# Cross-attention with a gated feed-forward layer: the second feed-forward weight converted in the second softmax stage by three engines, awaited chunk by chunk, and two slots of the attention output chain moved

## The reference

```
qh = (LN(x) @ Wq.T)    # 32 heads of 16; kh, vh from ctx: 8 groups, each used by 4 heads
attn = softmax(qh @ kh.T / 4)
x = x + (attn @ vh) @ Wfc.T + bfc
y = LN(x)                                     # fp8 (e4m3) products from here on
act = gelu(y @ w_gating[0]) * (y @ w_gating[1])   # 512 -> 2048, twice
out = x + act @ w_linear                      # 2048 -> 512
```

## Time and profile before

| | us |
|---|---|
| median of 3 runs | 476.73 |
| lowest and highest of them | 475.73, 479.82 |
| the profiled execution | 478.06 |
| its span, first to last instruction | 476.3 |

### The profile page before, as it was taken

One profiled execution on the slowest core, in us unless ns is written; L12 is line 12 of the kernel. 1 busy time (PEld: TensorE's weight loads), 2 busy tenths in 40 slices (PEclk: granted clock), 3 DMA queues, 4 the chain that ended last, 5 costly groups with the idle time before them and its releaser, 6 DMA issues.

```text
span 476.3 us, 11726 instructions
## 1 busy us (share of the span) xinstructions
PE 431.6 (91%) x4592; PEld 345.2 (72%) x4592; DVE 332.7 (70%) x688; ACT 314.6 (66%) x578; POOL 242.0 (51%) x227
## 2 busy tenths in 40 slices
PE   2977855889999999999999999999999999888997
PEld 2846744667797778877887778877887788557973
DVE  4587582886789667975888677966797578365442
ACT  5749862886459774787469755877479745775541
POOL 5679951589116950398027920696029810592000
PEclk9977977799999999999999999999999999899999
DMA  8878569653430454025601552034501250000001
GB/s 282 290 218 316 155 186 247 166 170 101 127 76 2 103 142 112 3 53 149 156 3 27 144 133 59 2 93 132 135 3 47 68 133 27 3 23 23 2 24 45
DMA packets 21720, 49.80 MB, mean 105 GB/s; under 512 B 5152, under 2 KB 5664, under 8 KB 21664
## 3 DMA queue, kind: packets, MB, share of 16 engines
q1 hardware_dynamic: 21376, 48.25, 36.0%
q10 hardware_dynamic: 288, 0.79, 0.6%
HBM read 23.86 MB, written 4.19 MB: 59 GB/s over the span
## 4 chain that ended last, share of the span: by engine, by line
PE 64%; DVE 10%; POOL 10%; issue 5%; DMA 4%; SPq 4%; ACT 3%; POOLq 0%; ACTq 0%; DVEq 0%
PE bank L627 17%; PE bank L647 10%; PE bank L435 7%; PE bank L436 6%; PE bank L437 6%; POOL plo L1242 6%; PE bank L538 5%; PE bank L505 4%; DMA stage<-in_w 3%; DVE mneg L1040 3%; PE bank L462 2%; PE bank L556 2%; PE bank L558 2%; SPq L349 2%; DVE osum L1053 1%
## 5 line engine op out<-in xcount | busy, mean ns | idle before, releaser
L1242 POOL TENSOR_TENSOR plo<-p,phi 128x512 f16<-128x512 f32 x128 | 152.6, 1208 | 49.5 <-ACT phi L822 49.0
L627 PE MATMUL bank<-x2T,wgate 128*128 128x128 fp8e4 x2048 | 130.9, 221 | 0.8 <-ACT x2T L834 0.8
L627 PEld LDWEIGHTS bank<-x2T,wgate 128*128 128x128 fp8e4 x2048 | 117.6, 99 | 14.2 <-issue 7.1
L1040 DVE TENSOR_REDUCE mneg<-bank 128x4 fp32r<-128x512 f32 x128 | 85.1, 685 | 21.3 <-PE bank L505 20.8
L819 ACT ACTIVATE p<-bank 128x512 f32<-128x512 f32 x128 | 77.6, 606 | 28.3 <-PE bank L538 27.6
L822 ACT ACTIVATE phi<-bank 128x512 f16<-128x512 f32 x128 | 77.5, 605 | 0.0
L647 PE MATMUL bank<-wlin,act 128*128 128x512 fp8e4 x256 | 74.4, 387 | 0.0
L845 ACT CAST ff<-bank 128x512 bf16<-128x512 f32 x64 | 37.4, 584 | 48.7 <-PE bank L627 48.7
L505 PE MATMUL bank<-kmask,cq 128*128 128x512 f32 x128 | 57.4, 480 | 6.1 <-DVE mneg L1040 5.4
L538 PE MATMUL bank<-qs,ks 98*128 98x512 f32 x128 | 55.1, 430 | 4.4 <-DMA qs<-mrow 2.5
L841 ACT ACTIVATE gate<-bank 128x512 bf16<-128x512 f32 x64 | 38.2, 597 | 31.1 <-PE bank L627 30.2
(11 more groups left out here) (111 smaller groups left out, 817.3 us busy)
## 6 DMA issues: line engine op xcount, KB each, us to landing
qs<-cq SPq DMA_DIRECT2D x90, 128.0 KB, 2.5
stage<-in_w SPq DMA_DIRECT2D x17, 512.0 KB, 6.3
ks<-khl SPq DMA_DIRECT2D x96, 64.0 KB, 2.0
cin<-in_ctx SPq DMA_DIRECT2D x8, 512.0 KB, 4.1
xr<-in_x SPq DMA_DIRECT2D x16, 256.0 KB, 3.7
out<-xr SPq DMA_DIRECT2D x16, 256.0 KB, 2.5
xr<-in_w SPq DMA_DIRECT2D x5, 512.0 KB, 4.6
kmask<-khl SPq DMA_DIRECT2D x28, 64.0 KB, 2.0
```

The source lines that it names most:

```text
L627: mm = pe.matmul(out[:, h * SEQ:(h + 1) * SEQ], wgate8[:, UH * v + h, kk, part, :], x2T[:, b % NB, kk, :], start=kk == 0, stop=kk == KT - 1)
L1040: dve.tensor_reduce(dst[:, :, 2 * half:2 * half + 2, j].rearrange("p a r -> p r a"), bank_of("S", q, i, s)[:, :].rearrange("p (r a k) -> p ...
L1242: pool.tensor_tensor(plo[:, e % PBUF, :], p32[:, e % P32BUF, :], phi[:, e % PBUF, :], ALU.subtract).then_inc(plo_ok, 1)
```

## The change

- Chunks 21 to 28 are converted in the softmax stage of pair 1: 21, 23, 25 and 27 by DVE at slots 3, 5, 8 and 11; 22, 24, 26 and 28 by POOL at slots 3, 5, 8 and 11 and by ACT two slots behind. The feed-forward part of pair 0 has no clamps and casts any more. Counts of conversions stay 11 by DVE and 13 by POOL and ACT.
- `down` of batch 0 waits at each slot for the chunk that it reads, and no longer for all.
- Places: chunks 17 to 28 go to `g0`, `g1`, `st0`, `st1`, then `st2`, `x6`, `st0`, `st1` twice.
- SP loads chunk 21 behind the context of pair 2, 22 to 24 behind all Q copies, and 25 to 28 in pair 1 ahead of `mask_k`.
- In pair 0 DVE converts its last two chunks a slot earlier (13 and 15), and `norm2_apply` and `turn_x2` come a slot earlier (17 and 18).
- In the last pair `turn_x2` and `x2_out` of batch 13 come at slot 14 and not at 11.

```diff
-W_PLACE += [("st0", "st1", "st2", "x4", "x6")[n % 5] for n in range(W_LIN - len(W_PLACE))]
-W_PLACE += [("st0", "st1", "st2")[n % 3] for n in range(CHUNKS - W_LIN)]
-W_DVE = [8, 10, 12, 14, 16, 18, 20] + list(range(W_LIN + 4, CHUNKS))
+W_PLACE += ["st0", "st1", "st2", "x4", "x6", "g0", "g1", "st0", "st1"]
+W_PLACE += [("st2", "x6", "st0", "st1")[n % 4] for n in range(CHUNKS - W_LIN)]
+W_DVE = [8, 10, 12, 14, 16, 18, 20] + list(range(W_LIN, CHUNKS, 2))
-CLAMP_SLOTS = (2, 5, 8, 10, 12, 14, 16)
-DVE_SLOTS = ((3, 5, 7, 9, 11, 14, 16), (1, 3, 5, 7))
+CLAMP_SLOTS = ((2, 5, 8, 10, 12, 14, 16), (3, 5, 8, 11))
+DVE_SLOTS = ((3, 5, 7, 9, 11, 13, 15), (3, 5, 8, 11))
-CHAIN_E = {True: dict(turn=13, project=(14, 14, 15, 15), residual=16, rstd=16, norm=17, turn2=19),
+LAST_TURN2 = 14
+CHAIN_E = {True: dict(turn=13, project=(14, 14, 15, 15), residual=16, rstd=16, norm=16, turn2=18),
...
                 stack_max(p, 1)
+                if p == 1:
+                    for c in range(W_LIN + 4, CHUNKS):
+                        load_chunk(c)
...
                         load_ctx(q + 1)
+                    if p == 0:
+                        load_chunk(W_LIN)
...
                         stack_q(q, hp)
-                        if p == 0:
-                            load_chunk(W_LIN + hp)
...
+                if p == 0:
+                    for c in range(W_LIN + 1, W_LIN + 4):
+                        load_chunk(c)
...
                     load_x(2)
-                    for c in range(W_LIN + PAIRS, CHUNKS):
-                        load_chunk(c)
...
-                    if b == 0:
-                        pe.wait_ge(w_conv, len(W_DVE))
-                        pe.wait_ge(w_cast, len(W_CLAMPED))
...
+                if b == 0:
+                    for c in range(W_LIN + lo // 2, W_LIN + (hi + 1) // 2):
+                        pe.wait_ge(*chunk_free(c))
...
-                    if n == chain["turn2"]:
+                    if n == (chain["turn2"] if q < NP else LAST_TURN2):
                         turn_x2(c_b)
...
-                    if first and n - 2 in CLAMP_SLOTS:
-                        chunk_cast(W_CLAMPED[W_AHEAD + CLAMP_SLOTS.index(n - 2)])
+                    if p < 2 and n - 2 in CLAMP_SLOTS[p]:
+                        chunk_cast(clamped.pop(0))
...
-                    if first:
-                        for c in W_CLAMPED[CLAMP_GATES + k:CLAMP_GATES + k + 1]:
-                            chunk_cast(c)
...
-                    if first and n in CLAMP_SLOTS:
-                        chunk_clamp(W_CLAMPED[W_AHEAD + CLAMP_SLOTS.index(n)])
+                    if p < 2 and n in CLAMP_SLOTS[p]:
+                        chunk_clamp(clamped.pop(0))
...
-                if first:
-                    for c in W_CLAMPED[CLAMP_GATES:]:
-                        chunk_clamp(c)
```

More of the change, by code:

```diff
@@ L55 @@
 W_AHEAD, W_FREE = 2, len(W_PLACE)
-W_PLACE += [("st0", "st1", "st2", "x4", "x6")[n % 5] for n in range(W_LIN - len(W_PLACE))]
-W_PLACE += [("st0", "st1", "st2")[n % 3] for n in range(CHUNKS - W_LIN)]
-W_DVE = [8, 10, 12, 14, 16, 18, 20] + list(range(W_LIN + 4, CHUNKS))
+W_PLACE += ["st0", "st1", "st2", "x4", "x6", "g0", "g1", "st0", "st1"]
+W_PLACE += [("st2", "x6", "st0", "st1")[n % 4] for n in range(CHUNKS - W_LIN)]
+W_DVE = [8, 10, 12, 14, 16, 18, 20] + list(range(W_LIN, CHUNKS, 2))
 W_CLAMPED = [c for c in range(W_GATE, CHUNKS) if c not in W_DVE]
-CLAMP_SLOTS = (2, 5, 8, 10, 12, 14, 16)
-CLAMP_GATES = W_AHEAD + len(CLAMP_SLOTS)
-DVE_SLOTS = ((3, 5, 7, 9, 11, 14, 16), (1, 3, 5, 7))
+CLAMP_SLOTS = ((2, 5, 8, 10, 12, 14, 16), (3, 5, 8, 11))
+DVE_SLOTS = ((3, 5, 7, 9, 11, 13, 15), (3, 5, 8, 11))
 W_PARTS = (2, 1, 1, 1, 1)
@@ L909, in _ @@
                 chunk_cast(c)
+            clamped = list(W_CLAMPED[W_AHEAD:])
             for p in range(NP):
```

## The result

| | before | after |
|---|---|---|
| median of 7 runs | 476.73 us (475.67 to 479.82) | 472.20 us (471.40 to 474.23) |
| ratio, 95% interval | | 0.9904 (0.9879 to 0.9929) |
| profiled execution, its span | 478.06, 476.3 us | 472.54, 470.7 us |
| first matmul of the units of pair 0 | 69.91 | 68.02 |
| start of the second softmax stage | 91.59 | 83.22 |

The change made the kernel 1% faster; 470.3 us had been predicted, with 466.5 to 475.5 as range. Two terms made that up, a gain ahead of the second softmax stage and a cost in it. Both came out larger than predicted: -8.4 us where -6.6 stood, and +3.0 where +0.2 stood. So it was in part luck that the number came nearly right: the two errors pull in opposite directions. Lines of the changed file are two to four higher than those of before.

The account below looks back on a forecast made before the run. PE, busy for 91% of the span, was taken as the bound. Queue -6.6 (the units' -1.0 inside it), second softmax stage +0.2 and last stage 0 gave -6.4: from the median 476.73 to 470.3 us, range 466.5 to 475.5.

Parts of the forecast that it names:

- Units of pair 0: First feed-forward part: its units start at 68.9 instead of 69.91 us, -1.0 (bounds -1.6 and +0.3).
- The stall chain: First feed-forward part: ACT's cast delays the copy of `ff`, then DVE's product, and PE waits 5.38 us for DVE's maxima.
- PE ready at 82.5: End of the first feed-forward part: DVE sets the pace, and PE is through at 82.5 us.
- The queue: SP's loads start 3.6 us earlier, maximum rows land behind chunk loads; second softmax stage starts at 85.0, not 91.59: -6.6.
- The stage: Second softmax stage: added conversions lengthen it, a shorter front gives back; together +0.2 us (bounds -0.9 and +2.5).
- First `plo` to the end of `rstd`: Second softmax stage: three POOL clamps ahead of `rstd` make it 19.0 to 20.3 us against 18.36, taken as +1.4.
- Behind `rstd`: Second softmax stage: POOL's fourth clamp is hidden by PE's slower slots; without that cover it costs 1.04 us.
- The last stage: Last pair: `turn_x2` moves from slot 11 to 14; POOL's queue hides it, 0 (bounds -0.3 and +0.3).
- POOL takes it back: Rival, chance 0.20: slower clamps and stretched `plo` cost +2.5 us in the second softmax stage; -4.1 in all, 472.6.
- the rows do not wait: Rival, chance 0.18: maximum rows do not wait for chunk loads, PE's 82.5 opens the second softmax stage; -8.2, 468.5 us.
- the round trip: Rival, chance 0.05: loads 25 to 28 wait for staging slots and land late in the second softmax stage; +2.6, 479.3 us.
- the stall stays: Rival, chance 0.07: DVE or a bank keeps the 5.4 us stall; only the earlier start remains, -1, 475.7 us.

Follow-up runs that it names:

- slots0: The changed kernel with only the first stage's slots put back (DVE's last two chunks, `norm2_apply`, `turn_x2`): 470.71 us, ratio 0.9877 to the kernel before.
- before_swap: The kernel before, with ACT's cast of each of chunks 21 to 24 behind its unit's copy of `ff` instead of ahead: 476.29 us, ratio 0.9971.
- rows_first: The changed kernel with the loads of chunks 22 to 24 moved behind the maximum rows and the x rows: 473.64 us, ratio 0.9888 to the kernel before.
- sp_held: The changed kernel with only SP's release put back, SP waiting for chunk 15's cast before the K copies: 476.79 us, ratio 1.0000 to the kernel before.
- release_only: The kernel before with only the late chunks' places changed, so chunk 20 waits for chunk 13; casts stay in the units: 473.08 us, ratio 0.9903.
- no_clamp: The changed kernel without POOL's four clamps in the second softmax stage; ACT's casts wait for the loads: 467.85 us, ratio 0.9759 to the kernel before.
- last11: The changed kernel with `turn_x2` of the last stage back at slot 11: 473.37 us, ratio 0.9927 to the kernel before.
- hold: The changed kernel with chunks 21 to 28 all converted by DVE and POOL waiting for `norm2_apply` after `norm2_rstd`: 469.99 us, ratio 0.9843 to the kernel before.

## Why the prediction was right, and where its steps were not

**Units of pair 0, predicted -1.0 (68.9).** Measured 68.02, -1.9, just outside its bounds; in other runs with the same slots 67.7 to 69.5. Over all profiles the prediction was right: 68.5 in the mean of the ten with these slots, 69.5 in that of the four with the old ones. slots0 shows that it matters little: 1.7 us later there, 0.3 at the stage. It is "inside" the queue's term, as the sum had it.

**The stall chain (ACT's cast, `ff`, DVE, PE).** The reading was right: with the casts gone no such wait is left, and in before_swap, with their order alone changed, it goes too. The step from it to a gain was not put as a term of its own, and rightly: what starts the stage is the rows.

**PE ready at 82.5.** It was ready at 83.22 - 2.20 = 81.0: 0.9 us from the earlier units (68.02 and not 68.9), 0.6 from the stretch behind, which took 13.0 us and not 13.6.

**The queue, predicted -6.6 (85.0).** Measured 83.22, -8.4, inside the bounds of -9.0 and -5.5. The mechanism held at each point: K copies at 56.55, context at 64.8, rows behind the chunk loads (rows_first took them out of there and the wait went), landing of the rows 4.5 us and not 1.8. The step that failed in size is the rate, "211 / 0.87 = 243 GB/s", taken for all of the 4.35 MB. Three windows show it, one of the kernel before and two of the changed one:

```profile
72.00:84.00 12.00, 6.62 (x71) 5.14 (x70) 3.93 (x7) 2.83 (x5) 2.08 (x2) 0.78 1.04 237
...
70.50:77.00 6.50, 6.41 (x80) 5.08 (x78) 4.50 (x9) 2.91 (x6) 1.27 (x1) 0.98 1.04 236
...
77.50:80.50 3.00, 2.94 (x38) 2.38 (x36) 2.97 (x6) 1.71 (x4) 1.27 (x1) 1.00 1.01 402
```

A full queue did move about 240 GB/s before, with the Q copies and chunk loads mixed, and it still does after, while the Q copies run. But the change puts three chunk loads in one piece behind them, and these alone move 402 (400 in sp_held, 395 in slots0). So chunk 24 landed at 81.6 and not at 84.4, -2.8; the second of the maximum rows landed 1.6 us behind it and not 0.5, +1.1. Together that is 1.7 of the 1.8 us that the term was short. The 265 GB/s of the longer window hold 0.5 MB of `x` as well, sent behind the rows. Why copies and loads that are mixed (237 before, up to 264 in release_only) move so much less than loads alone is not shown.

**The stage, predicted +0.2 (bounds -0.9 and +2.5).** Measured +3.04, outside. By its parts:
- Front: -1.2 predicted, -0.96 measured.
- First `plo` to the end of `rstd`: +1.4 predicted ("19.0 to 20.3, against 18.36"), +2.42 measured (20.78). The three clamps took 3.55 us, as the 3.1 to 4.4 had it. What failed is the base, "15.85 + 3.1 to 4.4": the 15.85 us are a regular stage's. Without clamps this stage takes 17.19 us to the start of `rstd` (no_clamp), 17.75 to its end, 1.9 more. POOL stands idle for 1.16 us of them and not for 0.33, mostly waiting for ACT's weights in the first slots, and is busy for 16.59 us with the same 16 instructions that take 15.52 in the regular stage.
- Behind `rstd`: 0 predicted. The clamp is hidden, as said. But behind the longer wait of PE ahead of it, 3.00 us and not 0.94, the clock was at its lower level for a part of the stretch (a mean of 0.85), 1.58 us. The prediction counted PE's wait and not what the clock does behind it; the row for that was in the trace of before: 211 GB/s stands beside a granted clock of 0.73 in the earlier trace rows, in a part with a wait of 5.4 us.

The Trainium skill (SBUF — State Buffer, Who interferes with whom) says that DVE in its two-port mode and GpSimd lock each other out for a whole instruction, which in the prediction would have added 2.1 us. Of the clamps one took 1.48 us and two 1.04, so being held up cost the three 0.4 us in all: the trace agrees in kind and not in size.

**The last stage, 0 predicted.** It was 0.1 by last11. The reason given, POOL's seven `plo` in one piece, is the one shown.

**The sum.** It is -8.37 + 3.04 - 0.2 = -5.5 us in the profiled executions, the -0.2 behind the units of pair 1, and -4.5 in the medians, against -6.4. Of the rivals, "POOL takes it back" (472.6) is nearest in time and in the stage's price; "the rows do not wait" fell, "the round trip" too (loads of the stage landed in 3.2 to 4.7 us, and PE waited for no chunk), and "the stall stays" fell by the waits. What the prediction did not ask is which half of the change pays. It took the casts' departure as the subject and the release as its help; the square of four kernels shows that the release alone is the gain, and that the casts' gain and price cancel.

**The scatter.** From the units of pair 1 to the end of the span release_only, no_clamp and slots0 took 350.4 us. The changed kernel took 351.9: 1.5 us more between two marks of the last stage (30.89 from `rstd` to `rstd`, against 29.35 in slots0), in a stretch with a clock of 0.52. Seven of the fourteen profiles have such a last stage (30.9), seven have not (29.3). The window of the changed kernel, and the like one of slots0:

```profile
405.10:408.60 3.50, 3.50 (x24) 2.15 (x24) 0.27 (x2) 2.89 (x7) 3.43 (x4) 0.52 0.03 7
```

```profile
405.30:408.00 2.70, 2.70 (x28) 1.72 (x27) 0.77 (x2) 2.60 (x7) 2.70 (x3) 1.00 0.03 6
```

Together with a stage now and then that loses 2.1 or 3.7 us to the held-up norm, this is as large as most differences of this study. The kernel before has such a last stage too (30.88). These events add up: before_swap, with one slow last stage and two held-up norms, took 357.8. A profiled span alone therefore does not rank two of these kernels; the stages read part by part and the medians do.

## What to carry to other kernels

When a change does two things at once, make the two kernels that do one each: here a single wait, released one place sooner by another choice of staging slot, was all of the gain, and the visible work on three engines was none. The work could be made to pay, once POOL had no clamps: hold has 0.9843 (0.9815 to 0.9871) against release_only's 0.9903 (0.9873 to 0.9934). Price a stage's added instructions on that stage without them, not on a regular stage, and where a wait of PE grows, look in the trace at what the granted clock did behind waits of that length. Do not carry a transfer rate from a stretch over to another mix of transfers: the same queue, full both times, moved 236 GB/s of Q copies and 402 of weight chunks. A removed wait is a gain only if nothing queued elsewhere ends the stretch: 2.3 us of PE's waiting in the last stage were worth 0.1.
